# Decoder layer, 32 sequences on one core: a rebuilt order of work, the loop unrolled, and normalising and quantising moved from VectorE to GpSimd

## The reference, cut to what matters

```python
def reference(x, ctx, mask, ...):
    x = x + attn(layernorm(x), ...)        # softmax(q k^T / sqrt(8) + relative bias) v, then w_out
    x = x + xattn(layernorm(x), ctx, ctx, mask, ...)   # masked softmax over the context
    x = x + ffn(layernorm(x), ...)
def ffn(x):                                # act_quant: per row, round(x * 127 / max|x|)
    gate = silu(act_quant(x) @ ternary(w_gate).T)
    up = act_quant(x) @ ternary(w_up).T
    return act_quant(gate * up) @ ternary(w_down).T
```

## Time and profile before

| | |
|---|---|
| time, median of 3 runs | 514.28 us (513.12 to 520.25) |
| span of the profiled execution, first to last instruction | 513.4 us |
| time of the profiled execution beside its span | not recorded apart; the two shortest runs are 513.12 and 514.28 us |
| TensorE, busy share of the span | 88% |
| VectorE | 78% |
| ScalarE | 73% |
| GpSimd | 50% |
| DMA engines, share | 44.4% |
| mean granted TensorE clock | 0.967 |

### The profile page before, as it was taken

One profiled execution on the slowest core, in us unless ns is written; L12 is line 12 of the kernel. 1 busy time (PEld: TensorE's weight loads), 2 busy tenths in 40 slices (PEclk: granted clock), 3 DMA queues, 4 the chain that ended last, 5 costly groups with the idle time before them and its releaser, 6 DMA issues.

```text
span 513.4 us, 18365 instructions
## 1 busy us (share of the span) xinstructions
PE 454.1 (88%) x5596; PEld 328.0 (64%) x5596; DVE 398.0 (78%) x1154; ACT 372.9 (73%) x993; POOL 254.6 (50%) x691
## 2 busy tenths in 40 slices
PE   2246889999999999999999999999999999997762
PEld 1224556777777777777777777777777777764440
DVE  5722446799888889888888988889888888877553
ACT  0222556788888888888888888888888887775451
POOL 4221445655565555555566655555556654434110
PEclk9999789999999999999999999999999999999785
DMA  6264255555455545454445555544454555223000
GB/s 186 77 192 107 72 143 142 140 142 141 134 134 144 141 122 145 139 135 131 122 138 135 135 128 135 137 135 122 133 137 137 137 137 136 79 86 92 23 7 10
DMA packets 82191, 62.48 MB, mean 122 GB/s; under 512 B 57634, under 2 KB 71714, under 8 KB 82146
## 3 DMA queue, kind: packets, MB, share of 16 engines
q1 hardware_dynamic: 82146, 61.92, 44.4%
HBM read 46.47 MB, written 14.88 MB: 119 GB/s over the span
## 4 chain that ended last, share of the span: by engine, by line
PE 78%; DVE 5%; DMA 4%; issue 4%; SPq 3%; ACT 3%; POOL 1%; DVEq 0%; POOLq 0%; ACTq 0%
PE bank L1117 14%; PE bank L1092 12%; PE bank L1059 11%; PE bank L1088 6%; PE bank L1055 6%; PE bank L1264 4%; PE bank L1210 3%; PE bank L1138 2%; PE bank L1237 2%; PE bank L1175 2%; PE bank L1154 2%; PE bank L1295 2%; PE bank L1303 2%; PE bank L1224 2%; PE bank L1196 2%
## 5 line engine op out<-in xcount | busy, mean ns | idle before, releaser
L533 ACT ACTIVATE probs<-bank 128x512 f32<-128x512 f32 x256 | 145.5, 597 | 32.0 <-PE bank L1092 31.7
L826 DVE TENSOR_REDUCE neg_max_S<-bank 128x4 f32<-128x512 f32 x128 | 87.1, 685 | 34.3 <-PE bank L1059 34.2
L826 DVE TENSOR_REDUCE neg_max_X<-bank 128x4 f32<-128x512 f32 x128 | 84.2, 676 | 8.9 <-PE bank L1059 5.7
L1059 PE MATMUL bank<-stack_k_S,stack_q_S 120*128 120x128 bf16 x512 | 46.9, 227 | 12.9 <-DMA stack_k_S<-scratch_S 12.4
L432 POOL TENSOR_TENSOR qk_rest_X<-qk_X,qk_parts_X 128x256 f32<-128x256 f32 x32 | 21.4, 670 | 70.8 <-ACT qk_parts_X L536 70.8
L1092 PE MATMUL bank<-stack_q_S,stack_k_S 122*128 122x128 bf16 x512 | 52.5, 229 | 4.5 <-DMA stack_q_S<-neg_maxT_S 4.5
L1117 PE MATMUL bank<-probs,v_aug_S 128*32 128x128 f32 x1024 | 55.5, 291 | 0.0
L1055 PE MATMUL bank<-mask_bias,ident_bf 128*128 128x512 bf16 x128 | 49.4, 386 | 3.6 <-issue 2.3
L1092 PEld LDWEIGHTS bank<-stack_q_X,stack_k_X 74*128 74x128 bf16 x512 | 40.6, 99 | 16.4 <-issue 1.6
L1092 PE MATMUL bank<-stack_q_X,stack_k_X 74*128 74x128 bf16 x512 | 50.8, 222 | 0.0
L1088 PE MATMUL bank<-ident_bf,mask_bias 128*128 128x512 bf16 x128 | 50.3, 393 | 0.0
(11 more groups left out here) (159 smaller groups left out, 1159.1 us busy)
## 6 DMA issues: line engine op xcount, KB each, us to landing
stack_q_S<-scratch_S SPq DMA_DIRECT2D x32, 288.0 KB
stack_k_S<-scratch_S SPq DMA_DIRECT2D x96, 96.0 KB
stack_q_X<-scratch_X SPq DMA_DIRECT2D x32, 288.0 KB
stack_k_X<-scratch_X SPq DMA_DIRECT2D x96, 96.0 KB
scratch_S<-qk_parts_S SPq DMA_DIRECT2D x32, 192.0 KB, 2.3
scratch_X<-qk_parts_X SPq DMA_DIRECT2D x32, 192.0 KB, 2.3
ctx_in<-ctx SPq DMA_DIRECT2D x32, 64.0 KB, 2.7
mask_in<-mask SPq DMA_DIRECT2D x32, 64.0 KB, 1.8
```

The source lines that it names most:

```text
L533: act.activation(probs[:, c, :], bank_b[c % 2][:, :], ACT.Exp).then_inc(sems["exp_" + a], 1)
L826: dve.tensor_reduce(neg_max[a][:, first_head(c):first_head(c) + 2 * HC - 1:2], bank_a[c % 2][:, :].rearrange("i (h j) -> i h j", h=HC), AX ...
L1059: last = pe.matmul(bank[:, part_of_bank(hh)], stack_q[a][rows, p, head(c, hh)], stack_k[a][rows, p, head(c, hh)], start=not masked, stop=n ...
```

## The change

The five `step` functions are written anew with other lags and another order; the loop is gone (every step is written out with constant semaphore values; the classes `Seq` and the registers go). `normalise` (three per step) and `quantise_y` (one) are issued by GpSimd; since its `tensor_scalar` adds a negated mean, GpSimd also gets `negate_mean`, three per step. The context comes transposed from the host, so its transposition on TensorE and the copy on ScalarE go. The value projections stand beside those of queries and keys (`project_qkv`). `neg_max_parts` is 128 columns wide instead of 32. `probs` and `o_raw` exist once per attention instead of once, and `v_aug` has 4 copies instead of 2. The transposed `xn_X` goes to bank 4, with `o`. The large load of x (24 sequences) is issued earlier in SyncE's queue.

```diff
-FRONT_S, A_S, B_S, FRONT_X, A_X, B_X, POST_X, FFN2 = 0, 2, 3, 4, 5, 6, 7, 8
-UNROLL = 4
-LOOP_FROM, LOOP_TO = 10, 30
+STEPS = [(t, t) for t in range(-2, B + 14)]
+V_COPIES = 4
...
-        v_aug = {a: sb(f"v_aug_{a}", [S, 2, H // 2, 4, 16]) for a in "SX"}
+        v_aug = {a: sb(f"v_aug_{a}", [S, V_COPIES, H // 2, 4, 16]) for a in "SX"}
-        neg_max_parts = {a: sb(f"neg_max_parts_{a}", [S, M_ROWS, H], BF16) for a in "SX"}
+        neg_max_parts = {a: sb(f"neg_max_parts_{a}", [S, 128], BF16) for a in "SX"}
-        probs = sb("probs", [S, CH, HC * S])
-        o_raw = sb("o_raw", [128, 2, S])
+        probs = {a: sb(f"probs_{a}", [S, CH, HC * S]) for a in "SX"}
+        o_raw = {a: sb(f"o_raw_{a}", [128, 2, S]) for a in "SX"}
...
-            for t in range(LOOP_FROM):
-                step(Step(0, t))
-            with eng.Fori(0, (LOOP_TO - LOOP_FROM) // UNROLL) as turn:
-                for t in range(UNROLL):
-                    step(Step(turn, LOOP_FROM + t))
-            for t in range(LOOP_TO, B + DEPTH):
-                step(Step(0, t))
+            for s, x in STEPS:
+                step(Step(s, x))
...
-                dve.tensor_scalar(xn[k][:], x_of(b), mv[k][:, 0:1], rstd[k][:, 0:1],
-                                  ALU.subtract, ALU.mult).then_inc(sems["xn_" + k], 1)
+                pool.tensor_scalar(neg_mean[k][:], mv[k][:, 0:1], -1.0, None, ALU.mult)\
+                    .then_inc(sems["neg_mean_" + k], 1)
...
+                pool.tensor_scalar(xn[k][:], x_all[:, b, :], neg_mean[k][:, 0:1], rstd[k][:, 0:1],
+                                   ALU.add, ALU.mult).then_inc(sems["xn_" + k], 1)
...
-                dve.tensor_scalar(y_q[:], xn["F"][:], y_inv[:, 0:1], ROUND16, ALU.mult, ALU.add)\
+                pool.tensor_scalar(y_q[:], xn["F"][:], y_inv[:, 0:1], ROUND16, ALU.mult, ALU.add)\
                     .then_inc(sems["y_q"], 1)
...
-                    pe.transpose(quarter(bank_s, 1), ctx_in[:, ctx_b.parity, :], ident[:])\
-                        .then_inc(sems["ctxT_ps"], 1)
...
-                pe.transpose(half_words.bitcast(BF16)[0:M_ROWS * H, :],
-                             neg_max_parts[a][:].rearrange("s m h -> s (m h)"), ident_bf[:])\
-                                 .then_inc(sems["maxT_ps_" + a], 1)
+                pe.transpose(half_words.bitcast(BF16), neg_max_parts[a][:], ident_bf[:])\
+                    .then_inc(sems["maxT_ps_" + a], 1)
...
+                attend("S", st, 3, 0, ("xnT_X", 4), ("o_raw_X", 7), ("o_raw_S", 4))
+                attend("S", st, 3, 1)
+                attend("S", st, 3, 2)
+                attend("S", st, 3, 3)
...
-    named = {"x": a["x"], "ctx": a["ctx_1024"], ...
+    named = {"x": a["x"], "ctx": a["ctx_1024"].transpose(0, 2, 1), ...
```

More of the change, by code:

```diff
@@ L373, in _ @@
+                max_in("X", st, 11)
+                parts_out("S", st, 6)
+                store(st, 14)
+            run(step)
             sp.wait_ge(sems["out_stored"], 16 * B)
@@ new lines, in add_shift, with rest @@
+            def add_shift(a, st, lag):
+                b = st.of(a, lag)
+                if b is None or (a == "S" and b == 0 and st is not START):
+                    return
+                pool.wait_ge(sems["xn_" + a], done(b))
+                pool.tensor_tensor(x_all[:, b, :], x_all[:, b, :], shift[a][:], ALU.add)\
+                    .then_inc(sems["shifted_" + a], 1)
+            def rest(a, st, lag):
+                b = st.of(a, lag)
+                if b is None:
+                    return
+                pool.wait_ge(sems["part1_" + a], done(b))
+                if b:
+                    pool.wait_ge(sems["part3_" + a], done(b - 1))
@@ L995, in _ @@
+                row_max("S", st, 2, 2)
+                row_max("S", st, 2, 3)
+                ln_stats("S", st, -2)
+            run(step)
         @block.tensor
```

1255 lines of the change are left out of this document (581 added, 674 removed).

## The result

The changed kernel takes 547.82 us, the median of four runs (543.26 to 549.74), beside 515.43 us (513.12 to 520.25) for the kernel before on the same chip: 1.061 times as long, 95% interval 1.054 to 1.069. I had forecast 482 us. Slower by 6%, where nine chances in ten stood on faster.

A forecast was written before the change was run, and what follows sets the result against it. TensorE was taken as bound by its own queue, losing much to switches between 32- and 128-column weights. A step falling from 13.27 to 12.06 us gave -29.0 us over 24 steps, the loop -2.5: 482 us, range 466 to 500.

The forecast's parts named there:

- item 7: TensorE's new waits, bounded by one at each of three normalised tiles: +0.15 us a step, bounds 0 and 0.6.
- Item 1, 2: TensorE, per full step: `attend` of S in one run, -0.70 us; transposition of the maxima with 128 columns, -0.40 us.
- Item 3, 4: TensorE, per step: value projection of X no longer alone, -0.15 us; the context's transposition gone, -0.11 us.
- Item 5: VectorE gives up the normalisations and `y_q`, 1.77 busy us a step; costed at nothing, since TensorE hides it.
- Item 6: GpSimd takes over normalisations, `y_q` and negated means: 0.66 us per moved `tensor_scalar`, 10.9 us a step, hidden but tight.
- Item 8: The loop written out: the longer fourth step goes, 0.5 us in 5 turns, -2.5 us.
- Item 9: Fill and drain of the pipeline: gains and losses sum to 0, with 5 us either way.
- C: Rival: GpSimd becomes the bound, its moved instructions slowed by sharing the memory side with VectorE; 535 us, chance 0.04.
- B: Rival: ScalarE and GpSimd get on the path, TensorE's delays return a step later; step 12.7, 497 us, chance 0.19.

The follow-up runs named there:

- e18: e17 with the normalisations and `y_q` back on VectorE, `xn_S` later in its queue; 487.58 us, 0.949 times the kernel before.
- e4: The kernel before with its loop written out, nothing else; 506.41 us, 0.986 times the kernel before.
- e17: The changed kernel with `stack_in` reading a same-size scratch written once at the start, without waiting for the scratch writes' landing; 499.01 us, 0.971 times before.
- e5: The changed kernel with the two scratch writes issued by GpSimd right behind `part3`, not by SyncE; 531.89 us, 1.032 times the kernel before.

## Why the prediction was wrong

**The step that failed is item 7, the new waits.** I bounded them by 0 and 0.6 us a step and took 0.15. They are 1.89, all for a DMA, and I had looked only at the three normalised tiles. Behind it stands an omission: I went through the queues of TensorE, VectorE and GpSimd, and of SyncE's I read neither how many us of a step its issues take (8.9 in before, 9.2 in after) nor what lies between a scratch write and the read of it. The trace of before and the new order of calls had both. With them, and the landing of 2.3 us of before, of which 0.4 us goes under the write's own issue and some 1.0 under the small ones behind it, each read stands for 0.9 us: 9.2 + 0.7 of gaps + 1.8 = 11.7 us of a step that I put at 12.06. No slack was left on that queue, and it was the one to bound from above. That the landing becomes 3.4 to 4.0 us, which by the same subtraction makes it 9.2 + 0.7 + 2.0 + 2.6 = 14.5 beside the 14.28 measured, no row of before shows; that scratch_X would be issued right behind the 576 KB, the order of calls does.

**Item 1, 2: right at their place.** `attend` of S 1.01 us, the maxima 0.06, in after as forecast. What I made of them, that TensorE is bound by its own queue so that what it saves the step saves, holds only while the next tile is ready: in the order of before, 0.62 us saved at their place gave 0.13 in an ordinary step, nothing in the mean of 24, and 5.6 us in all, which in the profiled executions come from the filling. It was no pure order of TensorE even in before; a full TensorE of the earlier trace rows and waits of 0.2 us do not show how little slack the others have.

**Item 3, 4: not tested alone.** The value projection takes the 0.22 us forecast at its place. Both are within e18, whose 12.48 us a step is 0.4 above the 12.06 of the sum. Even that flatters the sum: 0.25 of the 0.79 us below 13.27 is the writing out of the loop (e4), so items 1 to 4 together brought at most 0.54 us a step where 1.36 was forecast. That e18 comes within 6 us of 482 is in part luck, since the loop's larger gain makes up for it.

**Item 5: VectorE's relief is worth nothing, right,** and weaker than I had put it: in e18, at 12.48 us, VectorE has its old work back and is busy in 294.74 of 320 us, and the kernel is faster for it.

**Item 6: the load a little high, its hiding wrong.** `xn` takes 0.447 us on GpSimd and `y_q` 0.367, below my 0.66, and GpSimd is busy for 10.0 us of a step (223.91 of 320 us), not 10.9. Yet the 0.50 and 0.37 us that I had found for the chains and called hidden in full steps are not: 11 us in the order of after without its landing waits, 4 to 24 with them, 43 in that of before, of which the chain of F is 25. The Trainium skill, GPSIMD Engine Reference, section Performance versus the Vector engine, has about 2.6 cycles an element against 1 and 1.96 times the time for a `tensor_tensor`. That is another operation than ours: for this `tensor_scalar` the traces have 0.447 us against 0.347, 1.3 times, so the factor doesn't carry over, and the measurement decides.

**Item 8, the loop: right in sign, 2.5 forecast, 7.7 measured** (e4). I had priced the turn alone, and each straight step is shorter too, by 0.25 us. I had asked of the written-out steps of before only whether they are slower, and not read that the first two are faster.

**Item 9: not 0.** The filling is 7.7 us longer; e17, which keeps the early load of x, shows it to be the landings.

**The rivals.** The result is on the side of C, slower, but not by its mechanism: GpSimd has 30% idle time and its instructions did not suffer beside VectorE. B had the right form, a delay that comes back to TensorE a step later, with the wrong queue. No rival named SyncE, and none had the size but C, by another cause.

## What to carry to other kernels

When a change rewrites the order of several queues, do the sum for every queue that issues DMAs as for an engine: its issues per step, and for each wait what was put between the write and the read that needs it. Two engines' orders that bring forward or put back a tile by half a step can leave a DMA queue little under which to hide a landing; here every local reordering that was tried only moved the wait. To tell where a wait comes from, and not where it shows, take out the dependence, and leave the traffic and its place in the queue.

A tile that goes round TensorE and back in one step must be priced by the length of its chain, in order and with what stands ahead of it on the new engine; its duration and the engine's busy share say little. The same instruction cost nothing off that chain (`xn_S`) and a good part of 25 us on it (`xn_F`).

## What I had not expected of the hardware

A landing of 192 KB takes 2.3 us in before, where 3 us or more lie between the last issue of the 576 KB on the same queue and its own, 2.5 to 2.6 in e17 (1.6 us between), 3.0 to 3.2 in e18 (1.2), and in after 3.4 (0.9) and 4.0 (0.1). An issue of this write costs SyncE 0.37 us and GpSimd 0.92 to 0.94 (e5). A loop of four steps with waits on computed counts costs 0.25 us in every step beyond the 0.5 at its turn; which part of the loop does, no run separates. TensorE's clock fell to its lower level for 3.4 us behind stretches in which it mostly stood (147 to 150 us of after), so a wait of 2.6 us cost more than 2.6 us.
